# TensorE's order in the odd slots of the two stacks: mean and g columns ahead of the strips' sums

## The reference

```
qkv = shift_tokens(x) @ Wqkv             # 16 heads of 64
q, k = l2norm(q) * qs, l2norm(k) * ksc   # then rotary factors
sim = q . k within windows of 32 and the window before, masked, * 8
out = softmax(sim) @ v
x   = out @ Wo + x
xs  = shift_tokens(x)
mu, var = mean(xs), mean((xs - mu)**2)
xn  = (xs - mu) / sqrt(var + 1e-5) * g + bln
a, gate = split(xn @ W1 + b1)            # 341 columns each
x   = (a * gelu(gate)) @ W2 + b2 + x
```

## Time and profile before

| what | us |
|---|---|
| median of 3 runs (lowest, highest) | 4273.47 (4263.32, 4281.32) |
| the profiled execution's own time | 4269.46 |
| its span, first to last instruction | 4267.7 |
| TensorE matmuls busy | 3949.0 |
| VectorE busy | 3159.0 |
| ScalarE busy | 3073.6 |
| GpSimd busy | 1805.3 |
| mean granted TensorE clock | 0.956 of full speed |

### The profile page before, as it was taken

One profiled execution on the slowest core, in us unless ns is written; L12 is line 12 of the kernel. 1 busy time (PEld: TensorE's weight loads), 2 busy tenths in 40 slices (PEclk: granted clock), 3 DMA queues, 4 the chain that ended last, 5 costly groups with the idle time before them and its releaser, 6 DMA issues. The chain is left out here.

```text
span 4267.7 us, 112951 instructions
## 1 busy us (share of the span) xinstructions
PE 3949.0 (93%) x43857; PEld 2403.7 (56%) x43857; DVE 3159.0 (74%) x4169; ACT 3073.6 (72%) x7076; POOL 1805.3 (42%) x1071
## 2 busy tenths in 40 slices
PE   7997999999999999999966689999999999999998
PEld 3443656655656656656536546666566565665664
DVE  5773877878877878778735468878787787887785
ACT  3555778777878878877762267887787777777876
POOL 3111444444444444444404534444444444444442
PEclk7998999999999999999976599999999999999999
DMA  2212444444443444444300044444444444444442
GB/s 44 32 22 68 105 112 104 109 101 103 111 104 92 117 105 102 107 104 103 76 10 3 3 114 114 112 94 116 104 97 110 99 109 97 105 110 103 96 103 50
DMA packets 232523, 380.81 MB, mean 89 GB/s; under 512 B 59364, under 2 KB 122336, under 8 KB 231688
## 3 DMA queue, kind: packets, MB, share of 16 engines
q1 hardware_dynamic: 231560, 372.20, 37.5%
q10 hardware_dynamic: 384, 0.79, 0.2%
HBM read 39.22 MB, written 1.05 MB: 9 GB/s over the span
## 5 line engine op out<-in xcount | busy, mean ns | idle before, releaser
L839 POOL TENSOR_TENSOR b_roll<-b_roll,b_sws 128x1024 f32<-128x1024 f32 x384 | 909.6, 2369 | 1726.7 <-DMA b_sws<-b_roll 1726.7
L1205 DVE SCALAR_TENSOR_TENSOR b_roll<-ps,b_qks,b_rot 128x1024 f32<-128x1024 f32 x768 | 960.3, 1277 | 51.5 <-issue 27.4
L1118 ACT ACTIVATE b_prob<-ps,b_nmx 128x96 f32<-128x96 f32 x3072 | 752.8, 371 | 0.9 <-DVE b_nmx L1234 0.4
L1254 DVE TENSOR_TENSOR y<-ps,y 128x512 f32<-128x512 f32 x384 | 265.4, 691 | 526.4 <-PE ps L934 526.4
L844 POOL TENSOR_TENSOR b_prob<-b_prob,b_rinv 128x768 f32<-128x768 f32 x384 | 564.6, 1470 | 104.4 <-DVE b_rinv L1268 104.0
L881 PEld LDWEIGHTS ps<-ident,b_prob 128*128 128x128 f32 x3072 | 382.5, 141 | 301.1 <-issue 246.3
L881 PE MATMUL ps<-ident,b_prob 128*128 128x128 f32 x3072 | 467.4, 275 | 50.2 <-issue 34.7
L1072 ACT ACTIVATE b_pT<-ps 128x512 f32<-128x512 f32 x768 | 462.9, 603 | 50.6 <-PE ps L881 50.6
L1012 PE MATMUL ps<-b_wqkv,b_xs 128*128 128x256 f32 x1536 | 433.8, 405 | 12.9 <-DVE b_roll L1205 12.9
L1097 ACT ACTIVATE b_oT<-ps 128x512 f32<-128x512 f32 x384 | 227.5, 592 | 269.6 <-PE ps L902 253.4
L1265 DVE TENSOR_REDUCE b_ssm<-b_prob 128x8 f32<-128x768 f32 x384 | 363.5, 947 | 70.9 <-ACT b_prob L1118 70.9
(11 more groups left out here) (290 smaller groups left out, 6782.6 us busy)
## 6 DMA issues: line engine op xcount, KB each, us to landing
b_sws<-b_roll SPq DMA_DIRECT2D x1536, 128.0 KB, 2.3
b_vs<-b_va SPq DMA_DIRECT2D x384, 256.0 KB, 3.8
b_wqkv<-in_L_ffn_Wqkv SPq DMA_DIRECT2D x96, 192.0 KB, 3.7
b_xs<-y SPq DMA_DIRECT2D x126, 128.0 KB, 2.3
b_wo<-in_L_ffn_Wo SPq DMA_DIRECT2D x96, 64.0 KB, 3.1
b_xs<-y SPq DMA_DIRECT2D x42, 127.8 KB, 2.4
b_rot<-in_rot SPq DMA_DIRECT2D x2, 2048.0 KB, 8.1
b_w<-in_L_ffn_W SPq DMA_DIRECT2D x24, 170.5 KB
```

What stands on the lines that cost most here:

```text
L839: pool.tensor_tensor(prc[:, r, :, :], prc[:, r, :, :], sws[:, r % 2, :, :], ALU.add)\
L1118: g = act.activation(prob[:, kc, i, P - KEYS:P], wide[0][:, h * CH + m * KEYS:h * CH + (m + 1) * KEYS], ACT.Exp, bias=nmx[:, kc % 2, i:i + 1])
L1205: dve.scalar_tensor_tensor(out=two_runs((2 * r + i) * CH, (8 + 2 * (r % 2) + i) * CH), in0=both, scalar=scale, in1=rot[:, 2 * i:2 * i + 2, ...
```

## The change

In `slot` of TensorE in the stacks, the call of `strips` moves from ahead of the wait for `y_add` and the block of lines 975, 978 and 984 to directly behind that block, ahead of the waits for the masks. No instruction is added or removed, and no other engine's order changes.

```diff
@@ -966,8 +966,6 @@
                             m = pe.matmul(bank[2][:, :], w2[:, i, :], hid[:, i, :], start=(i == 0), stop=(i == FT - 1))
                         m.then_inc(S["f_out"], 1)
-                    if a and j % 2:
-                        strips(U, b)
                     if e and step in (0, 1, 2, 3, 4):
                         pe.wait_ge(S["y_add"], ONE + UE + 1)
@@ -982,6 +980,8 @@
                         if fk == 0:
                             pe.wait_ge(S["ffw_ld"], ONE + 208 * (L0 + f[0] + 1))
                         pe.matmul(bank[3][:, :], w1[:, 1, i * P:(i + 1) * P], fin, start=True, stop=True).then_inc(S["f_g"], 1)
+                    if a and j % 2:
+                        strips(U, b)
                     if b:
                         pe.wait_ge(S["exp_done"], ONE + UB)
                         pe.wait_ge(S["kn_done"], ONE + UB + 1)
```

## The result

| | before | after |
|---|---|---|
| median | 4269.13 us (4 runs, 4263.32 to 4281.32) | 4334.13 us (4 runs, 4325.53 to 4337.78) |
| profiled execution, span | 4267.7 us | 4323.8 us |
| ratio | | 1.0146, interval 1.0116 to 1.0175 |

What follows compares the result with a forecast made beforehand. The prediction took TensorE's own work per slot to bound the kernel. Its terms, -13 + 43 + 20 + 14 = +64 us, gave 4333.5 against the profiled 4269.5, stated as 4334 us, range 4302 to 4358.

Steps and rivals of the forecast that it cites:

- What bounds: TensorE in the stacks: a slot is the sum of its own work, so added work or wait lengthens the program.
- Effect 1, the neighbours: TensorE, 44 slots of step 4 and 22 means: one edge between unlike tiles less, 0.20 each, 13 us gained.
- Effect 2, g of step 2: 44 slots: g waits for ScalarE's f_in with the strips queued behind it, 0.98 each, 43 us lost.
- Effect 3, the mean of slots 3 and 19: The mean waits for its transfers and the strips come on top: 20 us lost, bounds 10 and 22.
- Effect 4, the tail on ScalarE: 88 slots of steps 2 and 4: line 934 waits for ScalarE's line 1097, 0.16 each, 14 us lost.
- the tail hides: Rival: ScalarE's o is in time, so line 934 loses nothing: 4320 us, chance 0.17.
- The loop's turns: Rival: TensorE's stops at the layer loop's turns swallow the delay, no change: about 4291 us, chance 0.04.
- The clock: Rival: new stops lower TensorE's clock, 0.9 us in each of 66 slots, 60 us added: 4394 us, chance 0.03.
- no edge cost would be saved: Rival: edges between tiles cost by number, not kind, so the new neighbours gain nothing: 4347 us, chance 0.04.
- everything would start at once: Rival: g and the mean wait nowhere, so all 132 slots gain 0.20: 4243 us, chance 0.02.

Runs made afterwards that it cites:

- experiment 3: Kernel before, with only g of step 4 and the mean of slots 9 and 25 moved ahead of the strips: 4275.28 us, one execution.
- experiment 2: Kernel before, with only the mean of slots 3 and 19 moved ahead of the strips: 4301.71 us, one execution.
- experiment 4: Kernel after, with ScalarE reading g of steps 2 and 4 in the same slot ahead of its line 1078: 4324.63 us, one execution.
- Experiments 1: Kernel before, with only g of step 2 moved ahead of the strips: 4316.33 us against 4269.73, ratio 1.010.
- experiment 5: Kernel after, with ScalarE making f_in (line 1135) ahead of the exponentials: 4263.36 us.
- experiment 7: Kernel after, with f_in early, g of steps 2 and 4 read ahead of line 1078, mean of slots 3 and 19 between scores and values: 4227.96 us.
- experiment 6: Kernel after, with f_in early, g of steps 2 and 4 read ahead of line 1078, mean of slots 3 and 19 behind the strips: 4225.75 us.

## Why the prediction was right

The forecast was 4334 us and 4334.13 was measured; so close a hit is luck, since the four executions of after lie between 4325.53 and 4337.78, and the two profiled ones differ by 56 where the sum said 64. The terms are the better measure, and each can be read in slot lengths.

- *What bounds*: TensorE's own sum per slot. Right, with one exception. In the steady layers the slots 2, 15, 16 and the even ones from 4 to 14 and 20 to 30, which were not to change, kept their length to a hundredth, and every changed one moved by its own terms. In slots 17 to 19 GpSimd stops TensorE in some layers, before and after, which the prediction did not see: slot 18 grew by 2.8 us in all, but it did so by 4.0 in experiment 3, which has no new wait, and shrank by 0.3 in experiment 2, so it varies between executions and is not put down to the change.
- *Effect 1, the neighbours*: forecast -0.20 a slot, -13 us. Measured -0.19 to -0.20: slot 9, and slot 7 once its tail is taken away (experiment 4). The rows were right to stand against the reading of the Trainium skill (TensorE: Matmul & The Clock Gate, "Step-by-step: what each phase is for") by which loads of weights hide beneath the matmul ahead. In the rows above they do between like tiles (the load 0.43 ahead of g, 963 to g 0.86), and not behind the strips (the load with g, strips to g 0.99).
- *Effect 2, g of step 2*: forecast 0.98, measured 1.13 less the tail of 0.13, that is 1.00, in 44 slots. Experiments 1 and 5 show the cause from both sides.
- *Effect 3, the mean of slots 3 and 19*: forecast +20 us, measured +19 in the kernel after and +20 alone. Slot 3 lost 0.98 to 1.00. Slot 19 was not the same in all layers, as the sum had taken it: ten layers lost 0.70 to 1.02, and two nothing, because their means had waited 0.95 and 0.86 behind the strips already in the kernel before. The ten lost 0.91 on average where the sum had 0.85, which makes up for part of the two.
- *Effect 4, the tail on ScalarE*: forecast 0.16 in 88 slots, 14 us; measured 0.13, 11.6 us. This was the least certain term, and it was right in place and a fifth too large: line 934 started 0.06 late and took 0.07 longer. The wait had been put at 0.11, with the 0.15 from ScalarE's end to TensorE's start taken over from f_in; from 1097 to 934 it was 0.11 (1013.46 to 1013.57). Experiment 4 removed it alone.
- *The rivals*: that the tail hides is refuted by 0.13. The loop's turns did not take up the delay: slot 31, in which they lie, became shorter by 4 us in all, where 43 would have been needed, and in the profiles of the other kernels it differs from before by -4 to +2. The clock stayed at 1.00 over the stops; over the whole execution it was 0.958 after, 0.956 before. The rule on short idles between groups of matmuls (the Trainium skill, the same page, "A second HAM failure mode: psum-queue depth-cycling") does not bite here: 66 single stops of 1.1 to 1.6 us left the granted clock at 1.00.

With the measured terms the sum is -13 + 44 + 19 + 12 = 62, and the forecast's was 64. That no edge cost would be saved (4347) is refuted by experiment 3, and that everything would start at once (4243) by the waits of 1.44 and 1.57.

## What to carry to other kernels

Before an instruction group is moved ahead of another on the engine that bounds the kernel, look at what each one's start is released by: here the strips, in front of a wait that outlasted them or nearly so, cost next to nothing, and once behind it they cost their full length of 1.00 us. Ask the same of every case of a loop body by itself; here one moved call meant a gain in half of its 132 slots and a loss of about a microsecond in nearly all of the other half. Then see whether the wait's releaser can be moved: with ScalarE's f_in (0.7 us of work) earlier, the slots of step 2 went from 1.13 us longer than before to 0.54 shorter in the same order of TensorE. It took two more moves, of ScalarE's reading of g and of the mean of slots 3 and 19, to turn 1.5% slower into 1.0% faster.

## What was not expected of the hardware

A matmul that had to wait only 0.06 us past its turn cost 0.13 in all: line 934 took 0.53 to its successor in place of 0.46. The loads of its weights show a difference. Before, the load starts at 1003.39, 0.11 ahead of the matmul and while the transposes still run; after, it starts at 1013.53, behind the wait and 0.03 ahead of it. That the lost head start of the load makes the 0.07 fits these rows, but no run shows it alone.

And the list of waits of before put the strips' stop of 0.30 down to "issue", with no releaser, though it is a wait for ScalarE's square of q. In experiment 5 it vanished once g stood in that place. In every slot of before with this stop of 0.30 (5 and 19 among them) the square ends 0.10 ahead of the strips' start. And in slot 1 of the first stack's first layer, where the square ends 1.7 us later in the slot, the strips are as much later: they start 0.14 behind it after a stop of 0.78, and the timeline names the square:

```profile
406.20 0.60 ACT L1126 ACTIVATE b_sq<-ps 128x512 f32<-128x512 f32 x1 [0.95 <-PE ps L956]
...
406.94 1.07 PE L913 MATMUL ps<-b_sq,b_head_of 128*32 128x512 f32 x8 [0.78 <-ACT b_sq L1126]
```

One thing stays open: in the five layers of experiment 7 in which slot 19 takes 9.58 to 9.62, and in four of experiment 6, the strips start 0.26 to 0.29 behind the square, which ends as early as ever. What holds them for the other 0.16 to 0.19 the profile does not show. A stop that the list calls "issue" can be a wait like any other.
